# Context handed over transposed, its first product moved, and scatters without waits in the second half

## The chip, the cores and the metric

The kernel runs on one core of a Trainium2 chip. The metric is the device time of one execution in microseconds (us). Engines: PE is TensorE (matmuls; PEld its weight loads), DVE is VectorE, ACT is ScalarE, POOL is GpSimd, SP is SyncE, which here only issues DMAs. TensorE's granted clock is given as a share of full speed: 1.00 is 2.4 GHz, 0.50 is 1.2 GHz.

## What is computed

Two layers over x of shape (8, 256, 256) with a context of the same shape, cut to what matters here:

```
x = x + xattn0(layernorm(x), ctx, ctx)      # gated attention, 8 heads of 32
x = x + ffn0(layernorm(x))                  # router: top 4 of 32 experts, and a shared expert
x = x + xattn1(ctx, layernorm(x), ...)      # long convolution of the context, two small FFNs
x = x + ffn1(layernorm(x))                  # 8 experts, all of them for every token

# xattn0: ig, fg = concat(q, k, v) @ gate weights;  q = layernorm(x), k = v = ctx
#         D = exp(log_D - max);  h = (q k^T / sqrt(32) * D) / normaliser @ v, normalised per head
# ffn0:   scores = softmax(x @ Wg); top 4; each token's row goes through its 4 experts
# xattn1: z = layernorm(ctx @ W_in + b_in); irfft(rfft(window * h) * rfft(z))
```

## The kernel before

Tokens are 16 tiles of 128 (`NT` = 16), the width is 256. Five instruction streams, one per engine, are written out by hand; each engine runs its own in order, and they are tied by semaphores only (`wait_ge`, `then_inc`). DMAs of one issuing engine form one queue. The stages, in order:

1. **Load and gates.** SP loads `ident`, the context `cx` (2 MB), `x` in two halves of 1 MB and `bcv`; ACT loads small constants (`const_loaded` counts ten of them and `bcv`). Token rows go to partitions by a rearranged view of the DRAM tensor, so each piece is one row of 1 KB. SP then writes 12.6 MB of zeros to the slot buffer `slots_in` in DRAM. PE transposes the context (`mix_turned(cx, j)`, L1684), ACT copies it to `kT` (L1175), PE forms the gates' share of the context (`gates(kT, b, 2)`, L1690), and then does the same for the normalised rows `xn` (to `qT`). DVE spreads `id2` into `sel` (L504), takes the statistics of x (L461), writes `xn` (L515) and copies `cx` to `vext` (L517). ACT brings the gates out as `rg` (L1184), from which DVE makes `r1` (L520) and the decay rows.
2. **Head loop**, 64 heads: PE (L1730 to L1748), ACT (L1231), DVE (L603), with POOL masking queries into `qM` (L1539).
3. **Router.** PE forms the positional hidden layer (L1816) and the first of eight context products, `context_part(0)` (L1803, L1807), for the convolution; ACT copies it (`copy_context(0)`, L1226), squares the last batch of heads and normalises rows (`normalise_rows`, L1210), which wait for `rows_scaled` (DVE, L494). `spare(bank, count)` (L1677) are matmuls whose result nobody reads. Then come the rows' transposes (L1766), the filter's second layer (L1793), the router logits, the top 4 on DVE, the counts on PE (L1854) and context products 1 to 7.
4. **Scatters beside shared expert and convolution.** POOL sends 64 indirect DMAs (`scatter`, L1604), 4 x 16, each with 128 token rows of 1 KB, to `slots_in`; after each fourth it waits until all have landed. Between them POOL does `affine(2)` and `affine(3)` (L1616, L1617) on the context. PE, ACT and DVE run the shared expert and then the convolution: `spectrum(n)` (L1927), `spectrum_copy` (L1296), the product on DVE (L836 to L843), `inverse(n)` (L1943), `inverse_copy` (L1290), for n = 0 to 5. `spectrum(4)` is the first that needs `affine(3)`.
5. **Tile loop**, 48 pairs of slot tiles: ACT loads them (`load_pair`, L1321) once all scatters have landed and its own copies are done; PE works on them (L1966, L1986, L2005) with expert weights that POOL splits (`split_expert`, L1589, L1591) after its last scatter.
6. Gathers, the small FFNs, and the loop over the 8 experts (L1879, L1895, L1122 to L1141), which is the longest part.

Of the kernel before, what the change touches and what calls it, by code (L numbers as in the profile page):

```python
# [13 lines left out]
P = 128  # L14
# [36 lines left out]
def build(nc, dram, out_d):  # L51
    ctx = ExitStack()
    with ctx:
# [178 lines left out]
        def sem(name):  # L232
            return ctx.enter_context(nc.semaphore(name))
# [4 lines left out]
        ctx_loaded = sem("ctx_loaded")  # L238
        const_loaded = sem("const_loaded")
# [159 lines left out]
        def _(sp):  # L399
            xv = dram["x"].rearrange("b (h p) d -> p (b h) d", p=P)  # L400
            cv = dram["ctx"].rearrange("b (h p) d -> p (b h) d", p=P)
            sp.dma_start(ident[:, :], dram["ident"]).then_inc(ident_loaded, 16)
            sp.dma_start(cx[:, :, :], cv).then_inc(ctx_loaded, 16)
            for i in range(2):
                sp.dma_start(x[:, 8 * i:8 * i + 8, :], xv[:, 8 * i:8 * i + 8, :]).then_inc(x_loaded[i], 16)
# [44 lines left out]
        def _(dve):  # L450
# [52 lines left out]
            dve.wait_ge(id2_done, 1)  # L503
            dve.tensor_copy(sel[:, :, :], id2[:, :].unsqueeze(2).to_broadcast([P, 64, P])).then_inc(sel_done, 1)  # L504
# [9 lines left out]
            for n in range(NT):  # L514
                dve.tensor_scalar(xn[:, n, :], x[:, n, :], mv[:, n, 0:1], rs[:, n:n + 1], ALU.subtract, ALU.mult).then_inc(norm_done, 1)  # L515
            dve.wait_ge(ctx_loaded, 16)
# [650 lines left out]
        def _(act):  # L1167
# [9 lines left out]
            for j in range(8):  # L1177
                mix_copy(j, kT[:, j % 2, (j // 2) * 512:(j // 2 + 1) * 512])
            for j in range(8):
                mix_copy(8 + j, qT[:, j % 2, (j // 2) * 512:(j // 2 + 1) * 512])  # L1180
# [43 lines left out]
            def copy_context(b):  # L1224
                act.wait_ge(zlin_done, b + 1)
                act.activation(zn[:, b, :, :].rearrange("p r d -> p (r d)"), ps[:, (2, 5)[b % 2] if b else 4, :], ACT.Copy).then_inc(zlin_copied, 1)  # L1226
# [8 lines left out]
            copy_context(0)  # L1235
# [36 lines left out]
            act.activation(sc0[:, :, :], sc0[:, :, :], ACT.Exp).then_inc(exp_done, 1)  # L1272
            act.wait_ge(filtF_done, 1)
# [237 lines left out]
        def _(pool):  # L1511
# [30 lines left out]
            pool.wait_ge(mixT_copied, 16)  # L1542
# [55 lines left out]
            def scatter(count):  # L1598

                for _ in range(count):  # L1600
                    k, n = sent[0] // NT, sent[0] % NT
                    if n == 0:
                        pool.wait_ge(slots_done, k + 1)
                    pool.indirect_dma_start(xs_d, bass.IndirectOffsetOnAxis(ap=idS[:, n, k:k + 1], axis=0), xn[:, n, :], None,  # L1604
                                            bounds_check=TILES * P - 1, oob_is_err=False).then_inc(scattered, 16)
                    sent[0] += 1
                    if sent[0] % 4 == 0:
                        pool.wait_ge(scattered, 16 * sent[0])
# [63 lines left out]
        def _(pe):  # L1672
# [6 lines left out]
            def mix_turned(src, j):  # L1679

                g, c = j % 8 // 2, j % 2
                wait(pe, mixT_copied, j - 3)
                for t in range(4):
                    last = pe.transpose(ps[:, j % 4, t * P:(t + 1) * P], src[:, 4 * g + t, c * P:(c + 1) * P], ident[:, :])  # L1684
                last.then_inc(mixT_done, 1)
# [8 lines left out]
            pe.wait_ge(ident_loaded, 16)  # L1694
            pe.wait_ge(ctx_loaded, 16)
            for j in range(8):
                mix_turned(cx, j)
            pe.wait_ge(gatew_done, 1)
            pe.wait_ge(mixT_copied, 8)
            for b in range(B):  # L1700
                gates(kT, b, 2)
            for g in range(5):
                if g < 4:
                    pe.wait_ge(norm_done, 4 * g + 4)
                    mix_turned(xn, 8 + 2 * g)
                    mix_turned(xn, 9 + 2 * g)
                if g > 0:
                    pe.wait_ge(mixT_copied, 8 + 2 * g)
                    gates(qT, 2 * g - 2, 0)
                    last = gates(qT, 2 * g - 1, 0)  # L1710
# [86 lines left out]
            def context_part(b):  # L1797

                bank = (2, 5)[b % 2] if b else 4
                if b:  # L1800
                    wait(pe, zlin_copied, b - 1)
                    pe.wait_ge(turned_copied, 4)
                pe.matmul(ps[:, bank, :].rearrange("p (r d) -> p r d", r=2), one[:, :], zHL[:, :].unsqueeze(1).to_broadcast([2, 2, D]),  # L1803
                          start=True, stop=False, skip_group_check=True)
                for r in range(2):
                    for k in range(2):
                        last = pe.matmul(ps[:, bank, r * D:(r + 1) * D], kT[:, k, b * SEQ + r:(b + 1) * SEQ:2], Win[:, k, :],  # L1807
                                         start=False, stop=k == 1, skip_group_check=True)
                last.then_inc(zlin_done, 1)
# [9 lines left out]
            pe.wait_ge(ones_set, 1)  # L1819
            pe.wait_ge(bias_split, 1)  # L1820
            context_part(0)
            spare(3, 6)
            turn_rows(0)
            pe.wait_ge(zlin_copied, 1)
# [17 lines left out]
            expert_logits(3).then_inc(logits_done, 1)  # L1842
            pe.wait_ge(filt_done, 1)
# [433 lines left out]
```

## Time and profile before

| | us |
|---|---|
| median of 3 runs | 1808.43 (1802.43 to 1808.79) |
| the profiled execution | 1811.1 |
| its span, first to last instruction | 1809.3 |
| PE busy in the span | 1672.6 (92%) |
| DVE busy | 1211.7 (67%) |
| ACT busy, POOL busy | 472.6, 470.2 (26% each) |
| mean granted clock of TensorE | 0.964 |

The profile is of one execution. Busy time of PE includes the modelled ends of pipelined matmuls, so a busy PE is not one at its peak. A timeline row gives the start, the duration, the engine, the line and the operation with its output and inputs; in brackets stand the idle time of the engine before it and what ended it. An engine's idle time matters only where that engine is on the chain that sets the end.

### The profile page before, as it was taken

The page shows a single profiled execution, that of the slowest core. Times are in us where ns is not written, and L with a number is a line of the kernel's source. Part 1 is how long each engine was busy: PE and PEld are TensorE (multiplying, and loading weights), DVE is VectorE, ACT ScalarE, POOL GpSimd, SP SyncE. Part 2 cuts the span into 40 slices and gives each one's busy share as a digit, 9 for nine tenths or more (in the row PEclk, how much of TensorE's full clock was granted, in tenths as well). Part 3 has the DMA queues.
Part 4 walks back from the last instruction along what each step waited for, and adds up shares of the span by engine and source line. Part 5 has one row for each costly group of instructions (what it writes and reads, how often), then busy time and mean ns, then how long its engine had stood idle before and what let it go on. Part 6 is the DMA issues. An engine that isn't in the chain of part 4 may idle for free.

```text
span 1809.3 us, 29109 instructions
## 1 busy us (share of the span) xinstructions
PE 1672.6 (92%) x9764; PEld 1441.2 (80%) x9765; DVE 1211.7 (67%) x2502; ACT 472.6 (26%) x836; POOL 470.2 (26%) x355
## 2 busy tenths in 40 slices
PE   6999987698956778999999999999999999999998
PEld 5996663398854667888888888888888888888887
DVE  6467778566665776666676676676676676666765
ACT  3444331133422345321121121121111211211211
POOL 4373256688436501010010010010010110100100
PEclk9998998899976899999999999999999999999999
DMA  9200022288643200001000010010010010010001
GB/s 368 85 1 30 18 75 86 100 243 265 200 135 109 66 1 18 18 18 36 18 21 31 17 35 17 17 35 17 17 35 17 17 35 17 17 35 17 17 0 47
DMA packets 53828, 106.54 MB, mean 59 GB/s; under 512 B 6528, under 2 KB 37696, under 8 KB 53632
## 3 DMA queue, kind: packets, MB, share of 16 engines
q1 hardware_dynamic: 19920, 63.33, 10.4%
q10 hardware_dynamic: 27696, 25.51, 4.4%
q0 software_dynamic: 6144, 16.79, 2.9%
q8 instruction: 43, 0.70, 0.2%
q14 instruction: 25, 0.20, 0.0%
HBM read 69.96 MB, written 35.65 MB: 58 GB/s over the span
## 4 chain that ended last, share of the span: by engine, by line
PE 78%; DVE 6%; issue 5%; POOL 5%; DMA 4%; ACT 2%; SPq 0%; POOLq 0%; DVEq 0%; another core or an unknown queue 0%; ACTq 0%
PE ps L1879 39%; PE ps L1895 20%; PE ps L1986 4%; POOL slots_in L1604 2%; DMA slots_in<-xn,idS 2%; PE ps L2005 2%; PE ps L1730 2%; PE ps L2083 1%; PE ps L1966 1%; POOL yg L1643 1%; DMA x<-in_x 1%; PE ps L1731 1%; PE ps L1747 1%; PE ps L1748 1%; DVE st L461 1%
## 5 line engine op out<-in xcount | busy, mean ns | idle before, releaser
L1879 PE MATMUL ps<-xTH,wH 128*128 128x512 f32 x1024 | 402.7, 393 | 0.5 <-DVE hF L1122 0.5
L1879 PE MATMUL ps<-xTH,wL 128*128 128x512 f32 x1024 | 402.2, 393 | 0.0
L1879 PE MATMUL ps<-xTL,wH 128*128 128x512 f32 x1024 | 398.9, 390 | 0.0
L1269 ACT ACTIVATE sg<-ps 128x512 f32<-128x512 f32 x264 | 157.6, 597 | 883.0 <-PE ps L1879 882.1
L1122 DVE TENSOR_TENSOR hF<-sg,ps 128x512 f32<-128x512 f32 x256 | 175.8, 687 | 303.4 <-ACT sg L1269 303.3
L1576 POOL TENSOR_TENSOR wL<-wS,wH 128x1536 fp32r<-128x1536 f32 x32 | 112.0, 3499 | 937.3 <-ACT wH L1264 937.3
L1895 PE MATMUL ps<-wL,hH 128*128 128x256 f32 x1024 | 289.8, 283 | 0.0
L1895 PE MATMUL ps<-wH,hL 128*128 128x256 f32 x1024 | 289.7, 283 | 0.0
L1895 PE MATMUL ps<-wH,hH 128*128 128x256 f32 x1024 | 288.6, 282 | 0.5 <-DVE hL L1131 0.5
L1131 DVE TENSOR_TENSOR hL<-hF,hH 128x512 fp32r<-128x512 f32 x256 | 258.1, 1008 | 0.1
L1879 PEld LDWEIGHTS ps<-xTL,wH 128*128 128x128 f32 x1024 | 192.8, 188 | 42.1
L1141 DVE SCALAR_TENSOR_TENSOR x<-ps,cw,x 128x256 f32<-128x256 f32 x512 | 222.6, 476 | 1.0 <-PE ps L1895 1.0
L1879 PEld LDWEIGHTS ps<-xTH,wH 128*128 128x128 f32 x1024 | 193.8, 189 | 34.2 <-issue 0.6
L1879 PEld LDWEIGHTS ps<-xTH,wL 128*128 128x128 f32 x1024 | 193.7, 189 | 30.5
L1895 PEld LDWEIGHTS ps<-wH,hH 128*128 128x128 f32 x1024 | 195.5, 191 | 10.6 <-DVE hL L1131 0.7
L1895 PEld LDWEIGHTS ps<-wH,hL 128*128 128x128 f32 x1024 | 195.5, 191 | 9.9
L1895 PEld LDWEIGHTS ps<-wL,hH 128*128 128x128 f32 x1024 | 195.5, 191 | 0.0
L1125 DVE CAST hH<-hF 128x512 fp32r<-128x512 f32 x256 | 109.3, 427 | 37.1 <-PE ps L1895 28.4
L1604 POOL DMA_INDIRECT slots_in<-xn,idS x64 | 74.6, 1165 | 58.8 <-DMA slots_in<-xn,idS 29.0
L1986 PE MATMUL ps<-eHL,hH 128*128 x384 | 82.3, 297 | 2.2 <-POOL eHL L1591 2.2
L1643 POOL DMA_INDIRECT yg<-slots_out,idG x48 | 51.2, 1066 | 68.6 <-DMA slots_out<-yo 49.0
L603 DVE SCALAR_TENSOR_TENSOR Cm<-ps,Dm 128x384 f32<-128x384 f32 x64 | 35.7, 558 | 46.9 <-ACT Dm L1232 43.0
(379 smaller groups left out, 2534.5 us busy)
## 6 DMA issues: line engine op xcount, KB each, us to landing
wS<-in_w SPq DMA_DIRECT2D x32, 768.0 KB
slots_in<-eS SPq DMA_DIRECT2D x16, 768.0 KB, 20.3
eS<-in_wr SPq DMA_DIRECT2D x32, 384.0 KB, 3.9
xl<-slots_in ACTq DMA_DIRECT2D x48, 256.0 KB, 3.8
slots_out<-yo ACTq DMA_DIRECT2D x48, 256.0 KB, 3.3
cx<-in_ctx SPq DMA_DIRECT2D x1, 2048.0 KB, 10.6
x<-in_x SPq DMA_DIRECT2D x2, 1024.0 KB, 13.8
out<-x SPq DMA_DIRECT2D x4, 512.0 KB, 2.9
```

What stands on the lines that cost most here:

```text
L1122: dve.tensor_tensor(hF[:, b, :], sg[:, b, :], ps[:, 2 + b, :], ALU.mult).then_inc(mul_done, 1)
L1125: dve.tensor_copy(hH[:, b, :], hF[:, b, :]).then_inc(h_high, 1)
L1131: dve.tensor_tensor(hL[:, b, :], hF[:, b, :], f32(hH[:, b, :]), ALU.subtract).then_inc(h_low, 1)
L1141: dve.scalar_tensor_tensor(x[:, tile, :], acc, cw2[:, tile, bass.ds(it, 1)], x[:, tile, :], ALU.mult, ALU.add).then_inc(evac_done, 1)
L1269: act.activation(sg[:, b, :], ps[:, b, :], ACT.Silu).then_inc(silu_done, 1)
L1576: pool.tensor_tensor(blocks(wL, slot, plain), blocks(wS, slot, plain), f32(blocks(wH, slot, plain)), ALU.subtract).then_inc(w_low, 1)
L1604: pool.indirect_dma_start(xs_d, bass.IndirectOffsetOnAxis(ap=idS[:, n, k:k + 1], axis=0), xn[:, n, :], None, bounds_check=TILES * P - 1, o ...
L1643: pool.indirect_dma_start(slot_rows(n)[:, k, :], None, ys_d, bass.IndirectOffsetOnAxis(ap=idG[:, n, k:k + 1], axis=0), bounds_check=TILES ...
L1730: pe.matmul(ps[:, i % 2, 0:256], kT[:, c, t0:t0 + P], qM[:, i % 12, :], start=True, stop=True)
L1879: last = pe.matmul(ps[:, 2 * half + b, :], piece(w, s, slot, col, P), v[:, k, g * 512:(g + 1) * 512], start=q == 0, stop=q == 5)
L1895: last = pe.matmul(o, h[:, b, t * P:(t + 1) * P], piece(w, s, slot, col, D), start=(opens and t % 2 == 0 and q == 0), stop=(closes and q = ...
L1986: last = pe.matmul(ps[:, 2 + b, t * D:(t + 1) * D], h[:, b, (2 * t + k) * P:(2 * t + k + 1) * P], eFlat[:, bass.ds(off + (w + k * D), D)], ...
```

## The change

The host hands over `x` and `ctx` already laid out by partition, and besides them the context transposed (`ctxT`), which is loaded straight to `kT` ahead of x; the plain `ctx` comes behind x. The context's transposes on PE and their copies on ACT go. DVE writes `sel` after `xn` instead of before the statistics. `context_part(0)` moves behind the router logits, with its copy behind the router's Exp, and 18 spare matmuls stand in its old place. POOL's waits after each fourth scatter stay for the first 32 scatters and go for the other 32. The diff, cut to its core:

```diff
@@ sync
-            xv = dram["x"].rearrange("b (h p) d -> p (b h) d", p=P)
-            cv = dram["ctx"].rearrange("b (h p) d -> p (b h) d", p=P)
             sp.dma_start(ident[:, :], dram["ident"]).then_inc(ident_loaded, 16)
-            sp.dma_start(cx[:, :, :], cv).then_inc(ctx_loaded, 16)
+            sp.dma_start(kT[:, :, :], dram["ctxT"]).then_inc(kT_loaded, 16)
             for i in range(2):
-                sp.dma_start(x[:, 8 * i:8 * i + 8, :], xv[:, 8 * i:8 * i + 8, :]).then_inc(x_loaded[i], 16)
+                sp.dma_start(x[:, 8 * i:8 * i + 8, :], dram["x"][:, 8 * i:8 * i + 8, :]).then_inc(x_loaded[i], 16)
+            sp.dma_start(cx[:, :, :], dram["ctx"]).then_inc(ctx_loaded, 16)
@@ vector
-            dve.wait_ge(id2_done, 1)
-            dve.tensor_copy(sel[:, :, :], id2[:, :].unsqueeze(2).to_broadcast([P, 64, P])).then_inc(sel_done, 1)
...
                 dve.tensor_scalar(xn[:, n, :], x[:, n, :], mv[:, n, 0:1], rs[:, n:n + 1], ALU.subtract, ALU.mult).then_inc(norm_done, 1)
+            dve.wait_ge(id2_done, 1)
+            dve.tensor_copy(sel[:, :, :], id2[:, :].unsqueeze(2).to_broadcast([P, 64, P])).then_inc(sel_done, 1)
             dve.wait_ge(ctx_loaded, 16)
@@ scalar
             for j in range(8):
-                mix_copy(j, kT[:, j % 2, (j // 2) * 512:(j // 2 + 1) * 512])
-            for j in range(8):
-                mix_copy(8 + j, qT[:, j % 2, (j // 2) * 512:(j // 2 + 1) * 512])
+                mix_copy(j, qT[:, j % 2, (j // 2) * 512:(j // 2 + 1) * 512])
...
-            copy_context(0)
             act.wait_ge(q_masked, B * NH)
             square(B - 1)
...
             act.activation(sc0[:, :, :], sc0[:, :, :], ACT.Exp).then_inc(exp_done, 1)
+            copy_context(0)
             act.wait_ge(filtF_done, 1)
@@ gpsimd
-            pool.wait_ge(mixT_copied, 16)
+            pool.wait_ge(mixT_copied, 8)
...
-                    if sent[0] % 4 == 0:
+                    if sent[0] % 4 == 0 and sent[0] <= 32:
                         pool.wait_ge(scattered, 16 * sent[0])
@@ tensor
-            pe.wait_ge(ident_loaded, 16)
-            pe.wait_ge(ctx_loaded, 16)
-            for j in range(8):
-                mix_turned(cx, j)
+            pe.wait_ge(kT_loaded, 16)
             pe.wait_ge(gatew_done, 1)
-            pe.wait_ge(mixT_copied, 8)
             for b in range(B):
                 gates(kT, b, 2)
...
-            pe.wait_ge(ones_set, 1)
-            pe.wait_ge(bias_split, 1)
-            context_part(0)
-            spare(3, 6)
+            spare(4, 18)
             turn_rows(0)
-            pe.wait_ge(zlin_copied, 1)
...
             expert_logits(3).then_inc(logits_done, 1)
+            pe.wait_ge(ones_set, 1)
+            pe.wait_ge(bias_split, 1)
+            context_part(0)
             pe.wait_ge(filt_done, 1)
@@ host
-    A["x"], A["ctx"] = I["x"], I["ctx_1024"]
+    A["x"], A["ctx"] = (I[n].reshape(NT, P, D).transpose(1, 0, 2) for n in ("x", "ctx_1024"))
+    A["ctxT"] = chunked(I["ctx_1024"].reshape(NT * P, D).T)
```

`context_part(0)` writes PSUM bank 2 instead of bank 4, like the other even ones.

## Rows read from the trace of the kernel before

**Rows 1.** The page's chain that ended last, by line, share of the span.

```profile
PE ps L1879 39%; PE ps L1895 20%; PE ps L1986 4%; POOL slots_in L1604 2%; DMA slots_in<-xn,idS 2%; PE ps L2005 2%; PE ps L1730 2%; PE ps L2083 1%; PE ps L1966 1%; POOL yg L1643 1%; DMA x<-in_x 1%; PE ps L1731 1%; PE ps L1747 1%; PE ps L1748 1%; DVE st L461 1%
```

**Rows 2.** Timeline of the start: start us, us, engine, line, operation [idle before <-releaser].

```profile
3.71 7.70 DVE L504 CAST sel<-id 128x8192 fp32r<-128x8192 f32 x1 [1.18 <-POOL id L1524]
...
18.06 7.15 PE L1690 MATMUL ps<-kT,gateW 128*128 128x256 f32 x32 [0.99 <-ACT kT L1175]
18.09 2.84 DVE L461 BATCH_NORM_STATS2 st<-x 128x6 f32<-128x256 f32 x8 [0.20 <-DMA x<-in_x]
...
24.69 5.26 DVE L515 TENSOR_SCALAR xn<-x,mv,rs 128x256 f32<-128x256 f32 x16
...
29.86 2.29 DVE L517 COPY vext<-cx 128x4096 f32<-128x4096 f32 x1
...
37.72 0.42 DVE L520 SCALAR_TENSOR_TENSOR r<-rg 64x256 f32<-64x256 f32 x1 [5.57 <-ACT rg L1184]
```

**Rows 3.** Windows (last columns: granted clock, DMA share, GB/s), then DMA issues (KB, us to landing).

```profile
12.00:15.00 3.00, 3.00 (x15) 3.00 (x16) 0.00 (x0) 1.45 (x3) 3.00 (x15) 1.00 1.11 342
159.00:161.50 2.50, 2.50 (x4) 0.28 (x2) 2.36 (x5) 0.00 (x0) 1.18 (x1) 0.50 1.02 409
...
cx<-in_ctx SPq DMA_DIRECT2D x1, 2048.0 KB, 10.6
...
tilen<-in_tilen ACTq DMA_DIRECT2D x1, 48.0 KB, 6.6
```

**Rows 4.** Timeline around the first context product, DVE, ACT and PE.

```profile
165.01 0.17 DVE L494 SCALAR_TENSOR_TENSOR sd<-mv,rs 128x8 f32<-128x8 f32 x1
...
166.57 0.60 ACT L1226 ACTIVATE zn<-ps 128x512 f32<-128x512 f32 x1 [10.71 <-PE ps L1807]
...
167.59 4.03 ACT L1210 ACTIVATE xn<-x,sd,rs 128x256 f32<-128x256 f32 x8
...
176.07 8.06 PE L1793 MATMUL ps<-Wp,h1T 128*128 128x256 f32 x24
```

**Rows 5.** Timeline of PE between logits and counts.

```profile
202.53 2.00 PE L1807 MATMUL ps<-Win,kT 128*128 128x256 f32 x8
207.09 0.38 PE L1854 MATMUL ps<-selm,tri 128*128 128x512 bf16 x1 [2.56 <-DVE selm L715]
```

**Rows 6.** Timeline of POOL: two scatters, and a gather behind sixteen unwaited ones.

```profile
229.56 0.98 POOL L1604 DMA_INDIRECT slots_in<-xn,idS  x1 [2.23 <-DMA slots_in<-xn,idS]
...
284.73 0.97 POOL L1604 DMA_INDIRECT slots_in<-xn,idS  x1 [0.30 <-issue]
...
549.91 1.12 POOL L1643 DMA_INDIRECT ya<-slots_out,idG  x1 [5.17 <-DMA yg<-slots_out,idG]
```

**Rows 7.** Scatters' second half: timeline, one window, line L840 (min/median/max ns).

```profile
303.11 3.20 POOL L1617 TENSOR_TENSOR zn<-zn,bcv 128x1024 f32<-128x1024 f32 x1
...
289.12 3.60 PE L1927 MATMUL ps<-zn,FZ 128*128 128x512 f32 x8
...
306.41 6.40 PE L1927 MATMUL ps<-zn,FZ 128*128 128x512 f32 x8 [6.38 <-issue]
...
306.00:308.00 2.00, 1.59 (x2) 0.83 (x3) 1.97 (x2) 0.00 (x0) 1.20 (x2) 0.50 0.00 0
...
308.69 0.69 DVE L843 TENSOR_TENSOR PI<-tv 128x512 f32<-128x512 f32 x1
...
318.37 0.69 DVE L839 TENSOR_TENSOR PR<-tv 128x512 f32<-128x512 f32 x1 [5.34 <-PE ps L1943]
...
L840 DVE TENSOR_TENSOR tv<-Zs,WG x6: 1224/1226/3253, 277.0 to 341.2; 128x1024 f32<-128x1024 f32 x6
...
351.26 2.06 ACT L1290 ACTIVATE dcw<-ps 128x512 f32<-128x512 f32 x4 [24.02 <-PE ps L1943]
354.36 1.96 ACTq L1321 DMA_DIRECT2D xl<-slots_in  x4
...
361.32 0.58 PE L1986 MATMUL ps<-eHL,hH 128*128 x1 [2.24 <-POOL eHL L1591]
```

More of the change, by code:

```diff
@@ L238, in build @@
         ctx_loaded = sem("ctx_loaded")
+        kT_loaded = sem("kT_loaded")
         const_loaded = sem("const_loaded")
@@ L1225, in copy_context @@
                 act.wait_ge(zlin_done, b + 1)
-                act.activation(zn[:, b, :, :].rearrange("p r d -> p (r d)"), ps[:, (2, 5)[b % 2] if b else 4, :], ACT.Copy).then_inc(zlin_copied, 1)
+                act.activation(zn[:, b, :, :].rearrange("p r d -> p (r d)"), ps[:, (2, 5)[b % 2], :], ACT.Copy).then_inc(zlin_copied, 1)
             for i in range(B * NH):
@@ L1677, in spare, with mix_turned @@
                     pe.matmul(ps[:, bank, 0:384], idb[:, :], maskT[:, :], start=True, stop=True)
-            def mix_turned(src, j):
-                g, c = j % 8 // 2, j % 2
+            def mix_turned(j):
+                g, c = j // 2, j % 2
                 wait(pe, mixT_copied, j - 3)
                 for t in range(4):
-                    last = pe.transpose(ps[:, j % 4, t * P:(t + 1) * P], src[:, 4 * g + t, c * P:(c + 1) * P], ident[:, :])
+                    last = pe.transpose(ps[:, j % 4, t * P:(t + 1) * P], xn[:, 4 * g + t, c * P:(c + 1) * P], ident[:, :])
                 last.then_inc(mixT_done, 1)
@@ L1704, in _ @@
                     pe.wait_ge(norm_done, 4 * g + 4)
-                    mix_turned(xn, 8 + 2 * g)
-                    mix_turned(xn, 9 + 2 * g)
+                    pe.wait_ge(ident_loaded, 16)
+                    mix_turned(2 * g)
+                    mix_turned(2 * g + 1)
                 if g > 0:
-                    pe.wait_ge(mixT_copied, 8 + 2 * g)
+                    pe.wait_ge(mixT_copied, 2 * g)
                     gates(qT, 2 * g - 2, 0)
@@ L1797, in context_part @@
             def context_part(b):
[L1799 to L1802, printed above, removed]
+                bank = (2, 5)[b % 2]
+                wait(pe, zlin_copied, b - 1)
+                pe.wait_ge(turned_copied, 4)
                 pe.matmul(ps[:, bank, :].rearrange("p (r d) -> p r d", r=2), one[:, :], zHL[:, :].unsqueeze(1).to_broadcast([2, 2, D]),
```

## The prediction

> **What bounds the kernel now.** I read the page first: the chain that ended last is for 39% and 20% the two matmul lines of the expert loop (L1879, L1895), but the scatter line L1604 with its transfers takes 4% of the span, and the wait for x 1% [rows 1]. The change touches nothing after the tile loop, so I count those stretches as fixed and read the timeline of three others.
>
> *Start.* x1 (the second half of x) is read at 18.09, as soon as it lands. VectorE's statistics, the normalised rows `xn` (to 29.95) and TensorE's transposes and gates follow without a gap, and VectorE then takes up `r1` at 37.72, which ScalarE's `rg` released [rows 2]. The head loop cannot start before this.
>
> *Between head loop and scatters.* ScalarE spends 166.57 to 167.2 copying the first context product, then squares the last batch, then normalises rows from 167.59. `rows_scaled` had been there since 165.18 [rows 4]. TensorE and VectorE both wait for those ScalarE steps, and the top-k work and the first scatter follow from them.
>
> *Scatters and convolution.* An indirect scatter holds GpSimd 0.97 us and the next follows 0.30 later (284.73), but after each fourth the gap is 2.23 us, for landing (229.56) [rows 6]. The filter convolution (PE, ACT, DVE) runs beside it and ends with ScalarE's copies at 353.32; the scatters let the tile loads go at 354.36 [rows 7]. So two chains end 1 us apart: speeding only the scatters is worth 1 us. They are coupled, though: `spectrum(4)` started at 306.41 after 6.38 us without work, when GpSimd's `affine(3)` (to 306.31) was done, and that one stands behind eight waited scatters. VectorE then waited 5.34 us for TensorE at 318.37 [rows 7].
>
> **The change part by part.**
>
> *A, the start.* Ahead of x1 lie as before 4.19 MB (2 MB context, 2 MB x), now in rows of 16 and 8 KB instead of 1 KB. With 1 KB rows the queue moved 342 GB/s in 12 to 15 us, and the first 2 MB took 10.6 us from issue; loads with long rows at 159 to 161.5 moved 409 GB/s [rows 3]. The difference of the late rates alone is 4.19 MB x (1/342 - 1/409), that is 2.0 us; the first half went slower than 342, so more can be won there. I take 3.0 for x1; bounds 0 (row length doesn't matter) and 4.5. The Trainium skill (DMA: Bandwidth & Descriptors, Where 436 GB/s comes from) holds that HBM binds such loads at some 358 GB/s for a core; by it the late difference is 0.5 us and the total 1.5 to 2.5 us less good, while the row at 409 is above it.
>
> Against this stands `sel`: its cast lasts 7.70 us and lay in VectorE's idle time (3.71 to 11.4). Now it stands between `xn` and `vext` (2.29 us). VectorE would be free at 29.95 + 7.70 + 2.29 = 39.94 instead of by 32.2, and `r1` waits: 2.2 us more than the 37.72 of before. TensorE meanwhile gains nothing from losing 32 transposes, as its gates wait for `xn`. The context's gates no longer wait for them, nor GpSimd's gate weights for `sel`; with `kT` there near 10 they run to about 17, as they need 7.15 [rows 2]. Then TensorE idles some 6 us before `xn`. After a gap of that length its granted clock was 0.50, the level of 1.2 GHz (306 to 308), and 8 matmuls took 6.40 us where 3.60 was enough before [rows 7]. Such a cold start costs between 0 and 2.8 us here; I take 2. It puts `rg` at about 39.7, beside the 39.94 of VectorE: it is covered, since the later of the two counts and not the sum. If `sel` were not the longer, it would cost the same 2. Sum of A: +2.2 - 3.0 = -0.8; bounds -2.3 and +2.5. The `ctx` load now lands after 6.3 MB, at 409 to 342 GB/s some 15 to 18 us and the start of the queue, near 20; `xn` and `sel` cover it up to 35. If it came later, each us would cost one. The added 2 MB push only the zero fill, whose first reader after the head loop comes at about 160.
>
> *B, the moved product.* ScalarE no longer copies it before `square(7)`, and `xn` starts when `rows_scaled` is there, 165.2 instead of 167.6 [rows 4]: -2.4. The 18 fillers in its place are TensorE's alone and end before the rows are ready. At its new place the product costs 2.00 us [rows 5] and its bias matmul, some 2.4 us on TensorE, behind the logits, where TensorE sat idle 2.56 us before the counts: covered, with about 0.1 left over. Its copy (0.6) falls in ScalarE's wait for the filter. Uncovered it would cost 2.4 and cancel the gain. Upside: the 24 filter matmuls took 8.06 us [rows 4], partly at the low clock; they take about 2.7 less if the fillers keep the clock up. I count nothing for that. Sum of B: -2.4; bounds 0 and -5.
>
> *C, the scatters.* The first 32 keep their waits. In the second half the 8 waits go. Would scatters without a wait choke? No row shows scatters so; the nearest is the gathers, of which 16 went out without a wait, and 5.17 us later the last had landed [rows 6]. So I cost a scatter at 1.28. Of the eight after `affine(2)` the second started at 284.73; seven more take it to 293.7, and one hold-up of 2 us by VectorE (below) to near 295.4. Before, `affine(3)` waited for landing till about 300.6 (its second operation starts at 303.11, the first takes 2.4). `affine(3)` then shares a port with VectorE: its two operations of about 2.4 us and VectorE's two-input operations hold each other off (L840 took up to 3.25 instead of 1.23 [rows 7]). In turn with them it ends at 303.0 instead of 306.3. VectorE's product 2 ends at 308.2 (before 309.4). `spectrum(4)` starts at 303.1, with an idle gap of 3 us and so probably at full clock, is out by 306.7; `inverse(2)` runs 308.2 to 313.7 instead of to 318.3. From there every step follows as before, 4.6 us earlier. The scatters: 303.8 + 24 x 1.28 = 334.5, and up to 6 us where VectorE's operations hold them up (2.0 as for L840, in three products): 340, landed by 343. So the bound passes to the convolution. ScalarE's copies end at 353.3 - 4.6 = 348.7; the loads went at 354.36: -5.6. At the loop's head the first L1986 waited 2.24 us for GpSimd's expert split [rows 7]; the split now starts at 340 and is ready, and the next to end is the low part of the first tile, some 1.6 us earlier. Sum of C: -7.2; bounds -2.7 (the convolution gains nothing: -1.0 and -1.6) and -10.
>
> Together -0.8 - 2.4 - 7.2 = -10.4. The profiled execution took 1811.1 (span 1809.3 and 1.8 around it), so it becomes 1800.7; the median of the runs shown is 2.7 lower, 1808.4, so I forecast 1798.0.
>
> **Rivals.**
>
> *The convolution keeps its pace* (`affine(3)` is held off by VectorE until about 306, or TensorE turns cold anyway). The coupling by the port speaks for it, VectorE's idle 5.34 us against it. C is -2.7, the total -5.9: 1802.5.
>
> *The start loses.* x1 lands no earlier and `sel` costs in full: A is +2.3, total -7.3, 1801.1. A further form: TensorE stays at 1.2 GHz for the whole x part, whose 9.9 us (from half of `xn`, 27.3, to the 37.2 before `rg`) would double; `rg` then passes `sel` by 7.5 us, the total is -2.9: 1805.5. The Trainium skill's page TensorE: Matmul & The Clock Gate (HAM oscillation) says that an idle gap re-throttles the array and the next products start cold; by that rule this form or my covered 2 us appears, and the rows agree that the clock fell in such a gap.
>
> *Slower: the constants come late.* ScalarE's small loads land 6.6 us after issue, beside 1 KB rows [rows 3]; all are there by 14, and `rg`, the fillers and the query copies need them by about 34. If each small packet had to wait behind one of 16 KB, the delay would grow with the row: 8 times 6.6 is 53 us, an end at 60 and a start 22 us late, 1820 in all. It decides from 37 us on, and cancels the gain at about 48. Against it: an engine has only some 40 long rows ahead of the zero fill.
>
> *The products speed up too*: the filter matmuls keep 2.4 GHz. B is -5, total -13: 1795.4.
>
> **How the numbers follow.** Forecast 0.48, convolution unchanged 0.20, start loses 0.14, clock bonus 0.12, slower 0.06. A measurement of this kernel can tell about 0.5%, 9.0 us, from no change, so the bound is at 1799.4; my forecast lies only 1.4 beyond it. Of the forecast's 0.48 I put 0.36 below it, all of the bonus, and 0.05 of the two small rivals: faster 0.53; the rest without the slow rival, 0.41, is the same; slower 0.06. The range reaches from B and C at their good ends (about 1790) to C unchanged with the start lost (-2.8, and the scatter of the runs): 1790 to 1807.
>
> **What would show it.** x1 read near 15 instead of 18.1; `sel` of 7.7 us after `xn`, and `r1` near 37; TensorE's clock at 0.5 where the x transposes start; rows normalised right behind `rows_scaled`; no idle time before L1854; unwaited scatters 1.28 apart; `affine(3)` done near 303 less the shift of A and B; the gap before that L1927 half as long; the tile loads released by ScalarE's last copy and no wait for L1591 at the first L1986. I am wrong if scatters without a wait take longer than 1.28 to issue, if constants gate `rg`, or if `counts` waits for the moved product.

## The result, and the profile after

| | changed kernel | kernel before |
|---|---|---|
| median, first session | 1814.85 us (1802.23 to 1816.45, 7 runs) | 1804.44 us (1801.58 to 1808.79, 7 runs) |
| ratio, 95% interval | 1.0035 (1.0018 to 1.0052) | |
| the profiled execution, its span | 1816.29, 1814.5 us | 1811.1, 1809.3 us |
| mean granted clock of TensorE | 0.961 | 0.964 |

I had forecast 1798.0 us in a range of 1790 to 1807. By the ratio the kernel became slower by 0.35%, inside the 0.5% that I had called no change, but the interval leaves out 1.000. The ratio is not the quotient of the two medians, which is 1.0058 (10.4 us). A later session gave the same kernel 1814.07 us against 1806.58 us before, with a ratio of 1.0010 (0.9984 to 1.0035); there the medians lie 7.5 us apart. The direction of the medians is the same in both; the size by the ratios is between nothing and 0.5%. What has to be explained is less that small loss than the 10.4 us of gain that did not come.

Each session has its own runs of the kernel before (medians 1804.44, 1808.47, 1806.58 and 1806.65 us), and two kernels are best compared within one session.

The page's chain that ended last no longer has the scatter line, which had 4% in [rows 1] with its transfers; the inverse product (L1936) has come in with 2%:

```profile
PE ps L1872 39%; PE ps L1888 20%; PE ps L1979 4%; PE ps L1998 2%; PE ps L1936 2%; PE ps L1920 1%; PE ps L1959 1%; POOL yg L1641 1%; PE ps L2076 1%; PE ps L2054 1%; DVE hL L945 1%; PE ps L1988 1%; DVE st L461 1%; DVE x L903 0%; DMA yg<-slots_out,idG 0%
```

I compared the two traces stage by stage. First the start, in the timeline of the changed kernel:

```profile
10.30 9.18 PE L1688 MATMUL ps<-kT,gateW 128*128 128x256 f32 x32 [10.30 <-DMA kT<-in_ctxT]
...
13.19 5.72 DVE L461 BATCH_NORM_STATS2 st<-x 128x6 f32<-128x256 f32 x16 [10.66 <-DMA x<-in_x]
...
22.66 5.25 DVE L513 TENSOR_SCALAR xn<-x,mv,rs 128x256 f32<-128x256 f32 x16
24.09 3.26 PE L1682 MATMUL ps<-ident,xn 128*128 128x128 f32 x16 [4.62 <-DVE xn L513]
27.84 4.42 DVE L515 CAST sel<-id 128x8192 fp32r<-128x8192 f32 x1
...
36.97 0.42 DVE L520 SCALAR_TENSOR_TENSOR r<-rg 64x256 f32<-64x256 f32 x1 [2.51 <-ACT rg L1182]
```

`xn` begins 2.0 us sooner than in [rows 2], `r1` 0.75 us sooner. Between head loop and scatters:

```profile
164.66 4.04 ACT L1208 ACTIVATE xn<-x,sd,rs 128x256 f32<-128x256 f32 x8 [1.61 <-DVE sd L494]
...
211.56 1.39 POOL L1602 DMA_INDIRECT slots_in<-xn,idS  x1 [13.63 <-issue]
```

ScalarE's rows are 2.9 us ahead of [rows 4]; the first scatter went out at 214.68 before, so steps A and B together had brought 3.1 us there in this pair of traces. Then `affine(3)` and the product that waited for it:

```profile
288.00 2.39 POOL L1614 TENSOR_TENSOR zn<-zn,bcv 128x1024 f32<-128x1024 f32 x1
290.46 2.35 POOL L1615 TENSOR_TENSOR zn<-zn,bcv 128x1024 f32<-128x1024 f32 x1
303.02 3.60 PE L1920 MATMUL ps<-zn,FZ 128*128 128x512 f32 x8
```

`affine(3)` is done at 292.81 us, 13.5 us sooner than in [rows 7], and `spectrum(4)` no longer waits or runs at half clock (3.60 us, not 6.40). VectorE takes up its sixth and last product at 330.00 us (before 334.17). Up to here the kernel is 4.2 us ahead. What follows, in the same timeline:

```profile
330.00 2.29 DVE L836 TENSOR_TENSOR tv<-Zs,WG 128x2048 f32<-128x2048 f32 x1
330.37 2.78 POOL L1602 DMA_INDIRECT slots_in<-xn,idS  x1 [0.30 <-issue]
332.33 1.23 DVE L837 TENSOR_TENSOR tv<-tv 128x1024 f32<-128x1024 f32 x1
333.16 1.72 POOL L1587 TENSOR_TENSOR eHL<-eS,zcol 128x768 fp32r<-128x768 f32 x1
...
336.11 5.36 PE L1675 MATMUL ps<-maskT,idb 128*128 128x384 bf16 x32
...
337.34 2.37 DVE L840 TENSOR_TENSOR tv<-Zs,WG 128x1024 f32<-128x1024 f32 x1
338.71 2.67 POOL L1589 TENSOR_TENSOR eHL<-eS,eHL 128x768 fp32r<-128x768 f32 x1
339.75 2.71 DVE L841 TENSOR_TENSOR tv<-Zs,WG 128x1024 f32<-128x1024 f32 x1
341.34 2.44 POOL L1587 TENSOR_TENSOR eHL<-eS,zcol 128x768 fp32r<-128x768 f32 x1
342.50 2.37 DVE L842 TENSOR_TENSOR tv<-tv 128x1024 f32<-128x1024 f32 x1
343.86 2.66 POOL L1589 TENSOR_TENSOR eHL<-eS,eHL 128x768 fp32r<-128x768 f32 x1
344.90 2.17 DVE L843 TENSOR_TENSOR PI<-tv 128x512 f32<-128x512 f32 x1
347.13 2.07 PE L1936 MATMUL ps<-PR,GI 64*128 64x512 f32 x2 [5.66 <-DVE PI L843]
...
356.92 0.60 ACT L1288 ACTIVATE dcw<-ps 128x512 f32<-128x512 f32 x1 [33.84 <-PE ps L1936]
357.08 0.41 ACTq L1319 DMA_DIRECT2D xl<-slots_in  x1
```

GpSimd is through with its scatters at 333.15 and starts at once on the expert splits; three experts' splits, six GpSimd operations, are allowed before the fourth waits for the sixth product. They and VectorE's product hold each other off. From L836 to the end of L843 the product takes 17.07 us; before it took 11.47 (334.17 to 345.64). TensorE has run its 32 fillers (`spare`, matmuls whose result nobody reads) by 341.5, then has nothing for 5.66 us where it waited 0.16 before, and its last inverse product takes 9.8 us (347.13 to ScalarE's first copy at 356.92) where it took 5.56 (345.70 to 351.26, [rows 7]). The granted clock, third from the end in these windows, is 0.50 there, which I call a cold TensorE below:

```profile
244.00:250.00 6.00, 4.58 (x19) 4.00 (x20) 5.63 (x17) 2.53 (x6) 3.14 (x4) 0.72 0.19 66
262.00:266.00 4.00, 1.96 (x9) 1.96 (x10) 3.90 (x5) 0.00 (x0) 3.36 (x3) 0.70 0.18 66
274.00:284.00 10.00, 7.94 (x12) 3.12 (x11) 9.69 (x8) 1.88 (x1) 8.12 (x6) 0.67 0.42 155
346.00:351.00 5.00, 3.87 (x6) 1.78 (x8) 1.07 (x1) 0.00 (x0) 4.29 (x4) 0.50 0.24 79
```

The account to this point: -4.2 at the product, +5.6 in it, +4.2 in the inverse product, so ScalarE's copies come 5.7 us late. The tile loads go only 2.7 us late (357.08 against 354.36), as no scatter is waited for any more, but from there to the tile loop's first matmul it takes 8.4 us where it took 7.0: that matmul is at 365.45 against 361.32 in [rows 7], +4.1. Why the loaded tiles come later behind their issue I can't say. The rest of the kernel adds 1 us in this execution.

The first three windows are a second find: TensorE at 0.67 to 0.72 in stretches where it had 1.00 before.

### The profile page after: what moved, and what is told of

It reads as the page before. It is cut to its first block, busy times and chain, and to the rows that moved or that the text cites. A ratio compares the mean times of both kernels' runs of the same rounds, so it can differ in the third digit from the quotient of the medians.

```text
span 1814.5 us, 29059 instructions
## 1 busy us (share of the span) xinstructions
PE 1678.7 (93%) x9745; PEld 1444.5 (80%) x9745; DVE 1207.0 (67%) x2502; ACT 469.6 (26%) x828; POOL 471.0 (26%) x355
## 3 DMA queue, kind: packets, MB, share of 16 engines
q1 hardware_dynamic: 16352, 65.43, 10.4%
## 4 chain that ended last, share of the span: by engine, by line
PE 74%; DVE 9%; issue 3%; ACT 2%; POOL 1%; DMA 1%; DVEq 0%; another core or an unknown queue 0%; POOLq 0%; ACTq 0%
PE ps L1872 39%; PE ps L1888 20%; PE ps L1979 4%; PE ps L1998 2%; PE ps L1936 2%; PE ps L1920 1%; PE ps L1959 1%; POOL yg L1641 1%; PE ps L2076 1%; PE ps L2054 1%; DVE hL L945 1%; PE ps L1988 1%; DVE st L461 1%; DVE x L903 0%; DMA yg<-slots_out,idG 0%
## 6 DMA issues: line engine op xcount, KB each, us to landing
x<-in_x SPq DMA_DIRECT2D x2, 1024.0 KB, 12.5
```

## The experiments

**Theory 1:** the splits collide with VectorE's last product, and TensorE turns cold behind it. **Theory 2:** scatters that don't wait slow the others themselves. **Theory 3:** the new start and the moved product bring TensorE to a lower clock between 245 and 290 us, and that is the loss. Each of the first four kernels had 12 runs; the kernel before had a median of 1808.47 us beside them (35 runs). The changed kernel was not in that session.

**e1, the split waits for the product.**

```diff
-                if e == 3:
+                if e == 0:
                     pool.wait_ge(prod_dve, 6)
+                if e == 3:
                     pool.wait_ge(zF_done, 6)
```

> The changed kernel, but GpSimd begins the split of the first expert's weights only when VectorE's sixth product is done. Theory 1 (the splits collide): the unwaited scatters let the splits of three experts (six operations with two SBUF inputs, 333.2 to 346.5) fall on VectorE's last product, whose four operations took 9.7 us in place of 4.5; TensorE was idle 5.66 us behind it and ran the last inverse product at a granted clock of 0.50. With the split behind the product, the four operations take about 4.5 us, PI is done near 341.8, the gap before the last inverse product is below 1 us, that product takes about 5.5 us in place of 9.8, and ScalarE's last copy ends near 347.5 to 348 in place of 359. What then goes late is the split itself: it starts near 341.8, and its first pair is ready near 346, before the tile loop's first product wants it, near 355. The tile loop begins 9 to 10 us earlier than in the changed kernel and the time falls by 7 to 10 us. Theory 2 (scatters without a wait slow VectorE, or their landing holds something): the four operations stay long and the time stays within 2 us of the changed kernel. Theory 3 (the loss is the clock of the stretch from 245 to 290 us, not the splits): the last product gets short here, but the kernel stays 5 us or more behind what that promises.

1807.54 us, ratio to before 0.9983 (0.9968 to 0.9999), 7.3 us below the changed kernel's first median and 6.5 below its second, both from other sessions. The timeline of e1:

```profile
335.87 1.22 DVE L840 TENSOR_TENSOR tv<-Zs,WG 128x1024 f32<-128x1024 f32 x1
...
339.65 0.69 DVE L843 TENSOR_TENSOR PI<-tv 128x512 f32<-128x512 f32 x1
340.40 1.12 PE L1937 MATMUL ps<-PR,GI 64*128 64x512 f32 x2 [0.16 <-DVE PI L843]
340.58 1.46 POOL L1587 TENSOR_TENSOR eHL<-eS,zcol 128x768 fp32r<-128x768 f32 x1
```

The product takes 11.36 us, the inverse product 5.56, the tile loads go at 346.12 in place of 357.08, and the late split is nobody's wait: the first tile matmul (353.21) waits for VectorE. Three scatters ran beside these operations and left them at 1.22, so theory 2 has no place here.

This trace does not show the added wait at work, though. Its scatters ended at 340.50, 7.3 us later than the changed kernel's and just behind the product's end at 340.34 (its `affine(2)` had begun at 274.82 and not at 268.79): without the wait the split would hardly have met the product either. The wait works in the traces of e7, e8, e9 and e12 below, which have it too: there GpSimd is through early and waits 4.8 to 23.7 us for the product. In e8:

```profile
338.02 1.23 DVE L840 TENSOR_TENSOR tv<-Zs,WG 128x1024 f32<-128x1024 f32 x1
...
342.73 1.46 POOL L1587 TENSOR_TENSOR eHL<-eS,zcol 128x768 fp32r<-128x768 f32 x1 [8.72 <-DVE PI L843]
```

GpSimd's last scatter ended at 334.01, the four operations are undisturbed, and the product takes 11.62 us. e8 also shared a session with the changed kernel (e5): 1804.60 against 1814.07 us, 12 runs each.

**e2, 70 fillers instead of 32** ahead of the last inverse product, with the collision left in.

```diff
-                    spare(0, 32)
+                    spare(0, 70)
```

> The changed kernel with 70 in place of 32 filler products ahead of the last inverse product, so that TensorE works on until VectorE's product is ready (32 took 5.4 us and ended 5.6 us too early). This keeps the collision on the port and takes away the cold TensorE alone. Theory 1: VectorE's four operations still take about 9.7 us, the last inverse product takes about 5.5 us in place of 9.8, and the time falls by about 4 us. If the cold clock is no part of the loss, the last inverse product takes 9 us again and the time is unchanged; if the fillers run past VectorE's product, the gain is smaller by the overrun, at most 0.7 us at full clock. Theory 2 and theory 3 expect the same 4 us or less from this and don't differ here.

1811.64 us, 1.0015 (0.9996 to 1.0034), between e1 and the changed kernel (4.1 us above e1 in the same session). The product still takes 17.07 us, and the fillers run right up to the inverse product, which now takes 5.56:

```profile
336.07 11.54 PE L1675 MATMUL ps<-maskT,idb 128*128 128x384 bf16 x70
...
347.54 1.12 PE L1936 MATMUL ps<-PR,GI 64*128 64x512 f32 x2
```

The loads go at 353.26, 3.8 us sooner; the fillers let the inverse product begin 0.4 later. So of the 9.8 us lost in the trace, 5.6 are the collision and 4.2 the cold engine behind it, and the second was shown by itself.

**e3, all waits back:** the new start and the moved product alone. **e4, the kernel before with the scatter edit alone.**

```diff
-                    if sent[0] % 4 == 0 and sent[0] <= 32:
+                    if sent[0] % 4 == 0:
```

> The changed kernel with the waits on landing after every fourth scatter in both halves again, so the new start and the moved context product alone. Theory 1: the start and the moved product are worth 3.1 us, as the two traces show at the first scatter, and nothing of it is lost later: 2 to 4 us below the kernel before, some 9 us below the changed kernel. Splits start near 351, after the last product, whose four operations take 4.5 us. Theory 3 (the new start or the moved product brings TensorE to a lower clock between 245 and 290 us): the products of the filter's up and down projections end no earlier than before (267.1), and the time is that of the kernel before or above it.

> The kernel before with one edit: the waits on landing stay for the first 32 scatters and go for the rest. Theory 1: the splits again start before VectorE's last product (about 336 against its 344) and the four operations take 9 to 10 us, the last inverse product runs cold; the time is 3 to 8 us above the kernel before, about that of the changed kernel or 3 us above it. Theory 3: without the new start and the moved product the stretch from 245 to 290 us keeps its clock, and the edit brings a gain or nothing.

e3: 1808.68 us, 1.0004 (0.9985 to 1.0024). e4: 1813.79 us, 1.0009 (0.9987 to 1.0031), its median 5.3 us above before, though its interval takes in 1.000. e4's trace has the collision again, in the same operations (this is the kernel before's code, so its line numbers):

```profile
340.69 2.37 DVE L840 TENSOR_TENSOR tv<-Zs,WG 128x1024 f32<-128x1024 f32 x1
342.06 2.66 POOL L1591 TENSOR_TENSOR eHL<-eS,eHL 128x768 fp32r<-128x768 f32 x1
...
350.47 2.07 PE L1943 MATMUL ps<-PR,GI 64*128 64x512 f32 x2 [6.78 <-DVE PI L843]
```

The scatter edit alone makes it, without the start. But e3's median did not come 3 us below before, and theory 3 may be partly right. Its trace is 3.4 us ahead at ScalarE's rows (164.2 against 167.59), its clock in the three windows above is 0.72, 0.69 and 0.67, and at the sixth product (332.67) it is only 1.5 ahead. At the first tile matmul (359.02) it is 2.3 ahead and its span 3.9 us shorter (1805.4 against 1809.3), so this one trace keeps most of a gain that the median of 12 runs doesn't show.

**e5, the changed kernel again,** and three kernels beside it (kernel before 1806.58 us).

> The changed kernel itself once more, beside the three kernels that follow, so that they can be set against it in one session. If the granted clock of the stretch from 245 to 290 us (0.50 in parts in the one trace of it) is chance, it need not show again; the splits beside VectorE's sixth product (9.7 us in place of 4.5), TensorE's wait of some 5.7 us behind it and the last inverse product at a low clock must show again in the same places. Time 5 to 10 us above the kernel with the late split.

1814.07 us, 1.0010. Everything showed again: product 17.07 us, inverse product 9.79, loads at 356.89. So did the clock: 0.72, 0.67 and 0.68 in the three windows, where I had thought of chance. Yet e1, whose code is the same up to 333 us, had 1.00 in all three in its one trace, in which ScalarE's rows came at 165.65 and not at 164.5 to 164.7; so it depends on more than the code. The low clock has a price: from the first scatter to the first spectrum behind the shared expert it takes 55.2 us in the changed kernel's trace (211.56 to 266.77) and 52.5 in e1's (212.77 to 265.24), as in the trace of before (52.4).

**e6, no scatter waits,** on top of e1.

```diff
-                    if sent[0] % 4 == 0 and sent[0] <= 32:
-                        pool.wait_ge(scattered, 16 * sent[0])
```

> The kernel with the late split (e1) and with the waits after every fourth scatter gone from the first 32 scatters too, so that no scatter waits for a landing. Theory 1: the scatters are not what ends last any more; VectorE's and TensorE's convolution is. Without the first eight waits the scatters of the first half end some 8 us earlier and the split still waits for the sixth product: within 3 us of e1. Theory 2 (scatters without a wait slow VectorE or the landing): more of them cost more, 3 us or more above e1, with VectorE's operations between 211 and 270 us longer than in the trace of the changed kernel.

1825.96 us, 1.0092 (1.006 to 1.0125), 6 runs, the kernel before at 1806.58: the slowest of all, against my own expectation. 32 scatters went out in a row from 212.84 to 254.3 us, 1.28 apart, and the other engines stood still (TensorE's 12.5 us are a wait for VectorE's `hL`, and follow from its stop):

```profile
242.15 0.35 DVE L763 COPY etf<-ps 1x192 f32<-1x192 f32 x1 [14.50 <-remote]
...
247.09 0.58 PE L1887 MATMUL ps<-sH,hH 128*128 128x256 f32 x1 [12.50 <-DVE hL L810]
...
258.51 0.60 ACT L1266 ACTIVATE sg<-ps 128x512 f32<-128x512 f32 x1 [29.15 <-remote]
```

The VectorE copy needs only a TensorE result, and in e1 it waits 2.60 us. VectorE's operations keep their lengths (a mean of 0.69 us for L663, as in e1), so they are not being held off as in the collision. The queue view of e6 for 212 to 262 us names one queue, for 262 to 275 the two that carry instructions as well:

```profile
q0 software_dynamic: 1536, 4.20, 23.5%
...
q8 instruction: 1, 0.02, 0.5%
q14 instruction: 1, 0.01, 0.1%
```

In e1 the same two packets come within 240 to 242 us. Engines that wait for nothing nameable while the instruction packets stay out look like a program that is not loaded; that is what the rows support, not what they prove, since no record says whose packet it is, and VectorE went on at 242.15, in the middle of the burst.

**e12, bursts of eight** in the first half, on top of e1.

```diff
-                    if sent[0] % 4 == 0 and sent[0] <= 32:
+                    if sent[0] % 8 == 0 and sent[0] <= 32:
```

> The kernel with the late split (e1), with a wait after every eighth scatter of the first 32 in place of every fourth. Without any wait there (e6) the scatters went out in one burst from 212.8 to 254.3 us, each still landed within 2.1 us, but VectorE stood still for 14.5 us, ScalarE for 29.1 us and TensorE for 12.5 us from about 228, waiting for nothing that the profile names, and no packet of the instruction queues came between 211.5 and 262.4 us, where e1 has two at 240.8. If a burst keeps program code from being loaded and a pause lets it through, bursts of eight leave pauses at 223, 235, 247 us: stalls of at most one burst (10 us) and as likely none, the instruction packets come in such a pause, and the time is within 5 us of e1, far below the 1826 of e6. If the number of scatters under way is what stalls the engines, eight already cost a third or more of e6's 18 us.

1807.05 us, 1.0006 (0.9990 to 1.0022), 10 runs, beside 1806.65 before. ScalarE stood still once, and went on in the pause between the burst that ended at 233.0 and the next at 235.27:

```profile
234.38 0.60 ACT L1266 ACTIVATE sg<-ps 128x512 f32<-128x512 f32 x1 [8.85 <-remote]
```

The stall is about as long as a burst, and ends in a pause; that is one case, and VectorE's in e6 ended without one. Its tile loads go at 350.8, 4.7 us later than e1's 346.1, and e6's at 370.9. The median doesn't show the 4.7 (1807.05 against e1's 1807.54, in another session); of e6 both show the loss.

**e8, the first context product back** at its old place, on top of e1.

> The kernel with the late split (e1) and the first context product back at its place ahead of the transposes of the rows, as in the kernel before. My step B says that the move is worth 2.4 us, all of it ahead of the rows' normalisation (165.6 us in the trace of e1, 167.6 before): 2 to 3 us above e1, with the normalisation and the first scatter later by that much. If the move costs at its new place what it saves at the old one, the time is that of e1.

1804.60 us, 0.9981 (0.9960 to 1.0002), no slower than e1 of the session before. Its trace shows the mechanism as I had it: ScalarE's copy at 165.87, its rows at 166.88 against 165.65, though its `r1` was 0.5 us sooner. But `context_part(0)` ran partly at the low clock (8 products in 3.63 us against 2.00 in [rows 5]) and the 24 filter matmuls behind it then came out at full clock, where e1's were partly cold (6.78 us against 8.00). So the first scatter goes out 174.7 us behind `r1` in e8 and 174.6 in e1: in this pair of traces the move is worth nothing there. At the sixth product e8 is 1.9 us behind e1 in the traces; the medians don't resolve that.

**e10, `sel` ahead of the statistics; e11, x in rows of 1 KB;** each the changed kernel with that one thing undone, one run each (1809.94 and 1810.57 us, which one run can't set apart from the others).

> The changed kernel with the cast sel back ahead of the statistics of x. I had priced its move at 2.2 us, from 7.70 us for the cast; behind xn it took 4.42 us. If its length depends on what runs beside it, it takes 7 to 8 us again at 3.7 us, beside GpSimd's memory sets, and VectorE is idle until x lands; VectorE is then free 4.4 us sooner behind vext, yet r1 is unchanged within 0.3 us (36.9), since it waits for ScalarE's rg and that for TensorE's gates. If the move did cost, r1 comes 1 us or more sooner.

> The changed kernel with x loaded from its own layout again, in rows of 1 KB, and all else the same. My step A held that long rows bring the second half of x 3.0 us sooner, 2.0 us of it by the rate (342 against 409 GB/s), half of which falls on x. If that is so, VectorE's statistics of the second half wait for it until about 15.5 to 16.5 us, and xn starts 1 to 3 us after the 22.66 us of the changed kernel. If the length of rows doesn't matter, xn starts at 22.7 again.

e10, timeline:

```profile
3.56 7.70 DVE L504 CAST sel<-id 128x8192 fp32r<-128x8192 f32 x1 [1.03 <-POOL id L1522]
...
7.06 4.30 POOL L1525 TENSOR_TENSOR gwt<-gwt 128x32 f32<-128x32 f32 x1
...
14.04 8.74 PE L1688 MATMUL ps<-kT,gateW 128*128 128x256 f32 x32 [14.04 <-POOL gateW L1528]
...
24.15 1.09 PE L1682 MATMUL ps<-ident,xn 128*128 128x128 f32 x8 [1.37 <-DVE xn L515]
...
35.74 0.52 DVE L520 SCALAR_TENSOR_TENSOR r<-rg 64x256 f32<-64x256 f32 x1 [5.57 <-ACT rg L1182]
```

`sel` takes 7.70 us there and 4.42 behind `xn`. `r1` waits for `rg`, not for `sel`, yet it comes 1.2 us sooner, so by my own condition the move did cost: ahead of the statistics `sel` delays GpSimd's gate weights to 14.04 (a small GpSimd operation, L1525, takes 4.30 us until the cast is over, where it takes 0.25 in the changed kernel), so the context's gates run later, TensorE is idle for 1.37 us in place of 4.62, and the x transposes are warm (1.09 us for eight in place of 3.26 for sixteen). In e11 the halves of x are read at 14.29 and 17.29, later than I had expected, and `xn` starts at 23.89: long rows are worth 1.2 us.

**e7 and e9, fillers where TensorE turns cold,** on top of e1. This is e9; e7 has 16 in place of 8, and nothing at `n == 1`.

```diff
+            for _ in range(8):
+                pe.matmul(ps[:, 6, 0:SEQ], gateW[:, 2, 0, :], kT[:, 0, 0:SEQ], start=True, stop=True)
             for g in range(5):
...
+                if n == 1:
+                    spare(6, 24)
-                if n == 5:
+                if n > 3:
                     pe.wait_ge(zF_copied, 6)
                     spare(0, 32)
```

> The kernel with the late split (e1) and two groups of fillers for TensorE: 16 small products between the context's gates and the first transposes of x (TensorE was idle for 4.6 us there, and the transposes then ran at a granted clock of 0.50 to 0.66), and 32 fillers ahead of the fifth inverse product (idle for 5.36 us, then 2.08, 1.91 and 1.68 us for pairs that take 1.02 to 1.12 warm, which held VectorE's sixth product up by 2.61 us). If a cold TensorE behind an idle gap is the cause of these, the two give 1 to 1.5 us and 2.6 us: 2 to 4 us below e1, with r1 near 36 in place of 37 to 38 and the fifth inverse product in 4 us in place of 6. Otherwise within 1 us of e1.

> A candidate: the kernel with the late split and fillers (e7), with 8 in place of 16 fillers at the start (the 16 ran to 25.83 us, while the first normalised rows were ready some 1.5 us sooner, and cost what they gained) and 24 fillers ahead of the second inverse product, where TensorE was idle for 5.02 us and then needed 6.3 us for what takes 4 warm. If warmth is what is missing there: r1 near 35.5 in place of 36.9, the second inverse product in 4 us, together 1 to 3 us below e7. If neither place is on the path that ends last, the time of e7, near 1803.

e7: 1802.88 us, 0.9970 (0.9949 to 0.9992), 12 runs. e9: 1797.45 us, 0.9950 (0.9925 to 0.9974), 8 runs, 9.2 us below the kernel before in its session, and the best of all. e9's timeline:

```profile
23.79 1.09 PE L1683 MATMUL ps<-ident,xn 128*128 128x128 f32 x8 [0.92 <-DVE xn L513]
...
35.38 0.42 DVE L520 SCALAR_TENSOR_TENSOR r<-rg 64x256 f32<-64x256 f32 x1 [1.24 <-ACT rg L1182]
...
292.36 4.06 PE L1676 MATMUL ps<-maskT,idb 128*128 128x384 bf16 x24
296.26 1.02 PE L1939 MATMUL ps<-PR,GI 128*128 128x512 f32 x2
```

`r1` is at 35.38, 1.6 us sooner than in the changed kernel (0.3 of it because `xn` began sooner); the second inverse product's first pair takes 1.02 us where it took 2.08 in the changed kernel, the fifth's 1.12 instead of 2.07. The loads go at 341.4, and the first tile matmul at 347.8.

## Why the prediction was wrong, by its own steps

**A, the start: sum right by luck, terms wrong.** Forecast -0.8, measured -0.75 in one pair of traces; in the eight traces that have the changed start as it is, `r1` comes between 36.62 and 38.27, so a sum of this size can't be read from one. I took 3.0 us for x; `xn` came 2.0 sooner, of which e11 gives 1.2 to the length of the rows. I took +2.2 for `sel` on VectorE; there it cost nothing, since it takes 4.42 us at its new place and VectorE was free 2.5 us before `rg`. The cold start of TensorE, which I had set at 2 us and covered by `sel`, is what took 1.2 to 1.3 us (e10, e9), and e10 shows that moving `sel` away from the start is what opened the gap ahead of it. The page TensorE: Matmul & The Clock Gate of the Trainium skill (HAM oscillation) says that an idle gap re-throttles the array and the next products start cold; by that rule, the traces agree, at 24.09 (4.62 us idle, then 0.58 over 24 to 28 us) and again at 347.13 (5.66 us idle, then 0.50). By the page DMA: Bandwidth & Descriptors (Where 436 GB/s comes from) of the Trainium skill such loads would be bound near 358 GB/s, a core's half of what one HBM stack gives to two cores; the changed kernel, on one core, moved 436 in this window, and the measurement decides:

```profile
12.00:16.00 4.00, 4.00 (x14) 3.29 (x14) 2.77 (x8) 0.00 (x0) 0.41 (x1) 1.00 1.05 436
```

**B, the moved product: right in the pair of traces, not borne out by the others.** -2.4 forecast, -2.4 measured between `r1` and the first scatter (-0.75 and -3.1). That the two agree is partly luck: from `r1` to the first scatter it takes 177.0 us in the trace of the kernel before, 175.6 in e4, whose code is the same up to there, 174.7 in e8 with the product at its old place, and 174.6 in the changed kernel. So B is worth between 0 and 2.4 there. Then TensorE stood at a low clock in the windows from 244 to 284 us and at the first spectrum behind the shared expert (266.77 against 267.08 us) only 0.3 of the 3.1 was left. I counted the clock as an upside of B alone; it was a cost of the stretch behind it.

**C, the scatters: the step that failed** is the sentence "the split now starts at 340 and is ready". C was to give -7.2; from the first scatter (-3.1) to the first tile matmul (+4.1) the trace has +7.2. The removal of eight waits was priced with what follows it on GpSimd at nothing. What kept the two apart before was only lateness: the split came at 354, when VectorE's last product was over. It moved to 333.16, and 5.6 us of collision plus 4.2 us of cold TensorE more than ate up what the product's start had gained. By my own figures, with A and B in them, the product would have run from 326.4 to 337.8 us and the split begun at 336.8: there was no margin, and I did not set the two beside each other. In the trace the one started 3.6 us later than that and the other 3.6 sooner. I had even used the same mechanism some sentences earlier, for `affine(3)` against VectorE's L840. The order in the trace is that of a lock: each operation ends about its own undisturbed length behind the end of the other engine's (L1587 at 338.63, L840 1.1 us later at 339.71, L1589 1.7 later at 341.38, L841 1.1 later at 342.46; alone they take 1.47, 1.23, 1.80 and 1.23). The page SBUF — State Buffer of the Trainium skill (SBUF: two separate sides) says that VectorE operations with two SBUF inputs and GpSimd operations that read SBUF take the shared pair in turn for a whole instruction; by that rule, the trace agrees. The split's start was too late in my sum because I let `affine(3)` end at 303.0 less A and B, 299.8; it ended at 292.8, and the 24 scatters behind it took 3.4 us longer than I had allowed.

The other term of C was too large by itself. I gave the convolution 4.6 us from the earlier `affine(3)`; the sixth product started 4.2 us sooner than before with A and B in it, 1.9 us sooner in e4 without them, and 2.7 sooner than in e3. VectorE and TensorE were the bound of most of that stretch.

**The rivals.** "The convolution keeps its pace" came nearest in kind, but its 1802.5 had the splits free too. "The start loses" and "constants late" did not happen (`ea` was made from its constants at 33.7). My one slower rival was in the wrong place (constants); the slower case was in C, and I had not asked what GpSimd does when it is early. With the collision removed the kernel ran at 1807.5 and, kept warm too, at 1797.5, close to what I had forecast without either; that is no confirmation, since the forecast had neither the wait nor the fillers in it.

The 0.5% bound held as a statement of size: both ratios are in it, and of the two intervals only the first session's leaves 1.000 out.

**Open.** Single executions of one kernel spread by 10 to 20 us (the changed kernel from 1800.21 to 1816.61 in e5, the kernel before from 1800.20 to 1819.91 beside it), and the clock between 244 and 284 us may be part of it. So may the collision: in e1's trace, whose code is the changed kernel's up to 333 us, the scatters ended behind the product, and an execution of the changed kernel that runs so would be spared it. That is argued; every trace of the changed kernel has the collision. What decides which executions are warm I can't say from one trace each. The spread limits every comparison here to some 3 us, and keeps A's and B's worth at the end unproved: e3 has both, and its median is that of before. What stops the engines in e6 is argued from rows, not shown.

## What to carry to other kernels

When a wait goes, follow the engine that becomes early past the work that was meant to gain: its next operations now run beside other ones, and where VectorE and GpSimd both read two tensors from SBUF, as here, they took turns. Order such work by the neighbour's semaphore and not by luck of lateness (one wait added: e1's median is some 7 us below the changed kernel's). Put fillers against the gap that is there in the new timeline; a number of fillers is tuned to one length of gap, and 32, which run for 5.4 us, were right before and useless for a gap of 11.

## What the hardware showed unexpectedly

- 32 indirect scatters issued 1.28 us apart without a pause stopped VectorE for 14.5 us and ScalarE for 29.15 us with nothing named as releaser, and the kernel's median was 19.4 us above the kernel before of its session (e6); with a pause after each eighth one stall of 8.9 us was left. The 24 unwaited ones of the second half did no such thing. The cause is not shown.
- The same cast (`sel`, 128x8192) took 7.70 us at 3.6 us of the run, beside GpSimd's memory set, and 4.42 us at 27.84 with GpSimd idle. In e10 that memory set ended at 6.98, and the cast 4.3 us behind it at 11.26, as if it had waited for it; GpSimd's L1525, begun at 7.06, ended at 11.36, right behind the cast.
- TensorE's granted clock between 244 and 284 us was 1.00 in the trace of before and of e1, but 0.67 to 0.72 in four traces (changed, e2, e3, e5) in which ScalarE's rows ahead of it were 2.9 to 3.4 us sooner than before. The others follow no single line: e4 0.89, 0.96 and 1.00; e7 0.72, 0.58 and 1.00; and e9, the fastest kernel, 0.78, 0.50 and 0.83.
